# Cross-attention and routed feed-forward attention: first-layer banks, the order at the start of the last stage, tables by kind, and seven batches of k gathered early

## The chip, the cores and the metric

One core of one Trainium2 chip runs the whole kernel in one launch. The metric is device time in microseconds of one execution, as the median of several. The engines are TensorE (PE, with its weight loads as PEld), VectorE (DVE), ScalarE (ACT), GpSimd (POOL) and SyncE (SP, which here only issues DMAs).

## What is computed

x and ctx are 16 batches of 256 tokens of 256 numbers, float32.

```python
x = x + xattn(layernorm(x), ctx, ctx, w_q, w_k, w_v, w_o)       # 16 heads, causal
xn = layernorm(x)
q, k, v = (fff(xn, *tree) for tree in ("q", "k", "v"))          # three trees
attn = softmax(q @ k.T / sqrt(256))
out = x + attn @ v
def fff(x, node_w, node_b, w1, b1, w2, b2):                     # each token goes to one of 16 leaves
    leaf = ...                                                  # 4 decisions, score >= 0
    return relu(x @ w1[leaf] + b1[leaf]) @ w2[leaf] + b2[leaf]  # 256 -> 64 -> 256
```

## The kernel before, in words

The kernel has four stages. Each engine has its own hand-written order; semaphores tie them together.

The attention stage (0 to about 400 us) goes batch by batch: cross-attention, layer norm, the routing decisions of the three trees, and an allocation that gives each token a row in xs_dram, sorted by leaf into pages of 128 rows. POOL scatters the normalised tokens there (indirect DMAs, 128 rows of 1 KB each). SP also loads the leaf tables: for tree 0 in `first_weights`, one of eight parts a batch, and for trees 1 and 2 in `load_table`, four parts each; two parts of tree 2 come during the feed-forward loop (after the stores of quads 3 and 7). A leaf's table row holds W2 = 128 numbers of the first layer and 257 of the second with a bias, side by side (WROW = 385); a part goes with one DMA for the first layer and two for the second.

The feed-forward loop handles 36 quads, 12 per tree, of four pages each. SP loads a quad's rows (`load_quad`, 512 KB) and stores its outputs (`store_quad`, 512 KB). PE's part per quad is `block_T` (transposes of xb, L816), `block_h` (first layer, L827) and `block_out` (second layer, L842 and L846). ACT copies the transposes (`copy_xT`, L1036), applies `relu` (L1043) and copies the outputs (`copy_y`, L1050). VectorE copies each page's leaf weights out of the tables (`take_weights`, L1401 and L1402). Quads go in pairs on PE: T, T of the next pair, out, out of this one, h, h of the next; ACT goes likewise with copy_xT, copy_xT, copy_y, copy_y, relu, relu. In the text a pass is one such turn of six blocks.

PSUM has eight banks, four pairs. Quads' transposes alternate between `pairs[0]` and `pairs[1]` (banks 0 to 3), outputs between `pairs[2]` and `pairs[3]` (banks 4 to 7), and the first layers use banks 4 and 5, the pair of the even quads' outputs. Hence block_h waits for the copy of the even quad's output (y_sb), and block_out for both quads' relus (h_sb).

POOL gathers the loop's outputs from ys_dram back into token order (indirect DMAs, one for 128 rows, L1606): all 32 of q, and then k for the first KB = 9 batches, 18 gathers. They start at quad 14; `after_sixth` ties each to an event of PE so that they are spread over the loop. k's first KFIRST = 5 batches count on one semaphore (k_in), later ones by pairs of batches (k_late).

The last stage is softmax attention over 16 batches, four buffers deep for v and x1 (U = 4): `transposes` of q and k (L877), `scores` (L888), `probs_T` (L898), `values` (L909) on PE; `copy_qT` (L1072) and `exps` (L1080) on ACT; `copy_kT` (L1419), `maxima` (L1424, L1428), `copy_pT` (L1434) and `finish` (L1445) on VectorE. PE starts it only when all outputs are copied (y_sb = 36), because these banks are the same eight. In `finals`, the step of batch b issues transposes of b + 2, probs_T of b, scores of b + 1, values of b - 1. POOL gathers the remaining rows of k (`late_row`, L1606) and all of v (`v_row`, L1638) beside it: first two late rows, the second after the first scores, then v's rows of batch 0, then in each step one late row and two rows of v. SP loads x1 (L503) after v's first rows have landed.

## Time and profile before

| | us |
|---|---|
| median of 3 runs (lowest, highest) | 662.35 (658.48, 664.43) |
| the profiled execution | 668.17 |
| its span | 666.2 |
| PE busy | 589.8 (89%) |
| DVE busy | 441.0 (66%) |
| ACT busy | 295.5 (44%) |
| POOL busy | 236.9 (36%) |
| DMA moved, mean rate | 169.58 MB, 255 GB/s |

Busy times overlap, so they don't add up; PE's is the sum over its instructions with modelled ends. The span is from the first to the last record of the profile, and the execution's time has about 2 us around it. "Releaser" or "<-" behind a row names what ended the engine's idle time before it; "remote" is an event whose sender the profile could not name. The granted clock is the share of 2.4 GHz that TensorE got: 1.00 is its upper level, 0.50 its lower one.

### The profile page before, as it was taken

Reading aid. Unit: us, or ns where it says so; the run is one execution under the profiler, and the core shown is the slowest. Engines: PE = TensorE matmul, PEld = TensorE weight load, DVE = VectorE, ACT = ScalarE, POOL = GpSimd, SP = SyncE. Lnnn points to the kernel's source line nnn. Section 1 sums busy time; section 2 is a strip of 40 time slices with the busy share of each in tenths; the row PEclk is TensorE's granted clock in tenths of the full one; section 3 lists DMA queues with packets and bytes.
Section 4 is the critical chain, followed back from the end, with each engine's and each line's share of the span. In section 5 each row is a group of like instructions: output and inputs, shape, how many; then the busy total and the mean of one; then the engine's idle time right before and its main releaser. Section 6 shows DMA issues by size and latency. Waiting matters only on the chain.

```text
span 666.2 us, 14743 instructions
## 1 busy us (share of the span) xinstructions
PE 589.8 (89%) x5131; PEld 505.4 (76%) x5131; DVE 441.0 (66%) x1511; ACT 295.5 (44%) x482; POOL 236.9 (36%) x298
## 2 busy tenths in 40 slices
PE   7578998998999999999899967759998888689996
PEld 6467787887888887878777856648887777579895
DVE  2765687887889888988788865564554544056664
ACT  3105454443445444545344532017886667333231
POOL 5700011223323432433233144540006556466642
PEclk8869999998999999999799988679999999799999
DMA  6798887889789988988867488758999998656663
GB/s 188 230 301 246 257 265 213 252 261 292 226 272 298 268 270 266 305 245 273 262 204 221 159 260 253 192 189 303 340 376 374 373 373 308 205 172 183 191 189 126
DMA packets 99639, 169.58 MB, mean 255 GB/s; under 512 B 12848, under 2 KB 67824, under 8 KB 99568
## 3 DMA queue, kind: packets, MB, share of 16 engines
q1 hardware_dynamic: 87712, 141.83, 67.7%
q0 software_dynamic: 9216, 25.18, 12.4%
q10 hardware_dynamic: 2640, 1.65, 0.9%
q8 instruction: 41, 0.67, 0.4%
q14 instruction: 30, 0.25, 0.1%
HBM read 92.59 MB, written 75.50 MB: 252 GB/s over the span
## 4 chain that ended last, share of the span: by engine, by line
PE 45%; SPq 16%; DMA 16%; issue 10%; DVE 6%; ACT 3%; another core or an unknown queue 2%; POOL 1%; ACTq 1%; DVEq 0%; POOLq 0%
DMA parts_dram<-k_lo 6%; SPq L334 6%; PE banks L827 5%; PE banks L816 4%; PE banks L888 4%; PE banks L842 4%; DMA parts_dram<-q_lo 3%; PE banks L547 3%; PE banks L909 3%; DMA k<-parts_dram 3%; PE banks L559 3%; PE banks L532 3%; DVE mneg L1184 2%; PE banks L682 2%; PE banks L877 2%
## 5 line engine op out<-in xcount | busy, mean ns | idle before, releaser
L1547 POOL DMA_INDIRECT xs_dram<-xn2s,place x96 | 95.3, 993 | 177.4 <-ACT pt L942 144.9
L942 ACT ACTIVATE pt<-banks 128x768 f32<-128x768 f32 x128 | 103.6, 811 | 108.8 <-PE banks L560 84.3
L1184 DVE TENSOR_REDUCE mneg<-banks 128x2 f32<-128x512 f32 x240 | 122.0, 550 | 37.3 <-PE banks L548 31.7
L547 PE MATMUL banks<-k,q 107*128 107x256 f32 x240 | 76.7, 371 | 18.9 <-DVE mneg L1184 9.0
L559 PE MATMUL banks<-q,k 109*128 109x256 f32 x256 | 75.3, 346 | 1.9 <-DMA q<-m_lo 0.2
L547 PEld LDWEIGHTS banks<-k,q 107*128 107x128 f32 x240 | 46.7, 195 | 30.3 <-DMA k<-parts_dram 11.1
L575 PE MATMUL banks<-pt,vp 128*32 128x256 f32 (+1 forms) x1024 | 54.9, 332 | 4.7 <-ACT pt L942 3.0
L560 PE MATMUL banks<-q,k 109*128 109x128 f32 x256 | 57.8, 226 | 0.0
L1606 POOL DMA_INDIRECT q_all<-ys_dram,place x32 | 31.3, 978 | 71.4 <-PE banks L816 52.6
L559 PEld LDWEIGHTS banks<-q,k 109*128 109x128 f32 x256 | 49.6, 194 | 6.7 <-ACT pt L942 5.9
L548 PE MATMUL banks<-k,q 107*128 107x128 f32 x240 | 54.4, 227 | 0.0
L560 PEld LDWEIGHTS banks<-q,k 109*128 109x128 f32 x256 | 50.4, 197 | 0.1
L1534 POOL TENSOR_SCALAR ve<-mv 128x2 f32<-128x2 f32 x32 | 7.4, 230 | 118.6 <-DVE mv L1110 79.5
L1036 ACT COPY xbT<-banks 128x1024 f32<-128x1024 f32 x36 | 34.9, 1018 | 30.8 <-PE banks L816 30.3
L1401 DVE COPY wb<-tables 128x128 f32 x96 | 21.0, 219 | 41.4 <-PE banks L846 33.3
L548 PEld LDWEIGHTS banks<-k,q 107*128 107x128 f32 x240 | 47.5, 198 | 0.5
L842 PE MATMUL banks<-wb,hT 64*128 64x256 f32 x288 | 42.4, 389 | 5.8 <-ACT hT L1043 3.3
L575 PEld LDWEIGHTS banks<-pt,vp 128*32 128x32 f32 x1024 | 26.8, 109 | 24.0 <-issue 6.0
L1050 ACT COPY yb<-banks 128x1024 f32<-128x1024 f32 x36 | 36.4, 1015 | 18.2 <-remote 11.3
L816 PE MATMUL banks<-ident,xb 128*128 128x128 f32 x288 | 37.5, 285 | 6.9 <-DMA xb<-xs_dram 6.9
L827 PE MATMUL banks<-xbT,wb 128*64 128x128 f32 x576 | 37.3, 282 | 5.1 <-issue 2.3
L827 PEld LDWEIGHTS banks<-xbT,wb 128*64 128x64 f32 x576 | 33.2, 142 | 10.2 <-issue 10.1
(177 smaller groups left out, 1310.5 us busy)
## 6 DMA issues: line engine op xcount, KB each, us to landing
ys_dram<-yb SPq DMA_DIRECT2D x36, 512.0 KB
xb<-xs_dram SPq DMA_DIRECT2D x35, 512.0 KB
k<-parts_dram SPq DMA_DIRECT2D x128, 128.0 KB, 4.3
q<-parts_dram SPq DMA_DIRECT2D x64, 256.0 KB, 4.2
xs_dram<-zero SPq DMA_DIRECT2D x45, 256.0 KB
xs_dram<-zero SPq DMA_DIRECT2D x18, 384.0 KB, 4.4
tables<-leafw SPq DMA_DIRECT2D x16, 257.0 KB
xt<-x SPq DMA_DIRECT2D x16, 256.0 KB
```

Source lines behind the costliest of these rows:

```text
L334: sp.dma_start(full[s][2 * DK * x:2 * DK * (x + 1), hs, :].bitcast(FP).rearrange("p h k -> p (h k)"), src).then_inc(stacked[r][s], 16)
L547: mm(ps[:, 0:S], q[0:KN, t, P:S], k[0:KN, t, :], start=True, stop=True)
L548: last = mm(ps[:, S:S + P], q[0:KN, t, 0:P], k[0:KN, t, 0:P], start=True, stop=True)
L559: mm(ps[:, 0:S], k[0:KM, t, 0:P], q[0:KM, t, :], start=True, stop=True)
L560: last = mm(ps[:, S:S + P], k[0:KM, t, P:S], q[0:KM, t, P:S], start=True, stop=True)
L575: last = mm(W_BANKS[par][32 * g:32 * g + 32, c * S + kt * P:c * S + S], vp[u][:, kt, t, :], pt[:, t, 0:S] if kt == 0 else pt[:, t, S:S + P ...
L816: last = nc.tensor.transpose(pairs[w % 2][:, c, m * P:m * P + P], xb[w][:, m, c * P:c * P + P], ident[:])
L827: last = mm(banks[4 + q % 2][e * HID:(e + 1) * HID, r * P:r * P + P], wb1[(2 * q + r) % UP][:, e, c * HID:c * HID + HID], xbT[q % 2][:, c, ...
L842: mm(pairs[2 + q % 2][:, e, r * D:r * D + D], hT[q % 2][half, r, :], wb2[(2 * q + r) % UP][half, 0:D], start=True, stop=False)
L942: nc.scalar.activation(pt[:, 2 * p:2 * p + 2, :], st_banks(b, p)[:, :, 0:S + P], ACT.Exp, scale=SC).then_inc(exp_sb, 1)
L1184: last = nc.vector.tensor_reduce(mneg[1 - u][:, t, 2 * j:2 * j + 2], S_BANKS[:, :, cols], axis=AX.X, op=ALU.max, negate=True)
L1547: gp.indirect_dma_start(xs_dram[tree], bass.IndirectOffsetOnAxis(ap=place[:, k:k + 1], axis=0), xn2s[m % RING][:, t, :], None).then_inc(sc ...
```

## The change

1. The first layers go to banks 2 and 3, the pair of the odd quads' transposes. block_h waits for both quads' xbT copies and no longer for yb. block_out waits for its own quad's relu. block_T of an odd quad waits for the relus of the pair before.
2. PE's and ACT's order at the start of the last stage: batch 0's transposes go ahead of the last two second layers, its scores right behind them, batch 1's transposes and scores follow, and the waits for yb come one by one before the first two probs_T. VectorE copies kT of batches 0 and 1 first and then takes the maxima.
3. Each table is two runs: all leaves' first layers, then all leaves' second layers.
4. KB = 7 and KFIRST = 3: 14 gathers of k in the loop. The 18 late rows come one and two by turns in the steps of the last stage, none ahead of v's first rows.

```diff
-KB = 9
-KFIRST = 5
+KB = 7
+KFIRST = 3
...
+        whole = [wl0[:]] + [tables[:, t * LEAVES * WROW:(t + 1) * LEAVES * WROW] for t in range(2)]
+        w1s = [w[:, 0:LEAVES * W2].rearrange("p (l n) -> p l n", l=LEAVES) for w in whole]
+        w2s = [w[:, LEAVES * W2:LEAVES * WROW].rearrange("p (l n) -> p l n", l=LEAVES) for w in whole]
...
-                sp.dma_start(wl[t][:, ls, 0:W2], leafw1[t, :, ls, :]).then_inc(wt_late[t], 16)
+                sp.dma_start(w1s[t][:, ls, :], leafw1[t, :, ls, :]).then_inc(wt_late[t], 16)
...
                 ge(pe, xbT_sb, q - 1)
+                if q % 2 == 1:
+                    ge(pe, h_sb, 2 * (q - 1))
...
-                ge(pe, y_sb, 2 * (q // 2) - 1)
+                ge(pe, xbT_sb, 2 * (q // 2 + 1))
...
-                            last = mm(banks[4 + q % 2][e * HID:(e + 1) * HID, r * P:r * P + P],
+                            last = mm(banks[2 + q % 2][e * HID:(e + 1) * HID, r * P:r * P + P],
...
-                pe.wait_ge(h_sb, 4 * (q // 2 + 1))
+                pe.wait_ge(h_sb, 2 * (q + 1))
...
-            pe.wait_ge(y_sb, Q)
...
+                    if i * U + u < 2:
+                        pe.wait_ge(y_sb, Q - 1 + i * U + u)
                     probs_T(i, u)
-                    if u + 1 < U or more:
+                    if (u + 1 < U or more) and i * U + u > 0:
                         scores(i + (u + 1) // U, (u + 1) % U)
...
                 if q + 2 < Q:
                     block_T(q + 2)
                     block_T(q + 3)
+                else:
+                    transposes(0, 0)
                 block_out(q)
                 block_out(q + 1)
...
             scores(0, 0)
             transposes(0, 1)
+            scores(0, 1)
...
                 if q + 2 < Q:
                     copy_xT(q + 2)
                     copy_xT(q + 3)
+                else:
+                    copy_qT(0, 0)
                 copy_y(q)
                 copy_y(q + 1)
...
-            copy_qT(0, 0)
+            copy_qT(0, 1)
             exps(0, 0)
-            copy_qT(0, 1)
...
+                    if i * U + u == 0:
+                        maxima(0, 1)
                     copy_pT(i, u)
-                    if u + 1 < U or more:
+                    if (u + 1 < U or more) and i * U + u > 0:
                         maxima(i + (u + 1) // U, (u + 1) % U)
...
             copy_kT(0, 0)
+            copy_kT(0, 1)
             maxima(0, 0)
-            copy_kT(0, 1)
...
-            gp.wait_ge(tq_ps, 1)
-            late_row(0)
-            gp.wait_ge(s2_ps, 1)
-            late_row(1)
...
+            late = 0
             for b in range(NB - 1):
-                if b + 2 < (NB - KB) * T:
-                    gp.wait_ge(tq_ps, min(b + 3, NB))
-                    late_row(b + 2)
+                for _ in range(1 + b % 2):
+                    if late < (NB - KB) * T:
+                        gp.wait_ge(tq_ps, min(b + 3, NB))
+                        late_row(late)
+                        late += 1
```

## Rows read from the trace of the kernel before

**Rows 1.** Stages: length; PE, PEld, DVE, ACT, POOL busy; clock; DMA share; GB/s
```profile
480.00:500.00 20.00, 19.71 (x232) 17.39 (x228) 10.22 (x48) 16.30 (x26) 1.14 (x2) 1.00 1.05 376
520.00:540.00 20.00, 17.90 (x210) 15.73 (x210) 10.29 (x48) 14.04 (x22) 12.12 (x14) 1.00 1.00 361
...
600.00:620.00 20.00, 20.00 (x121) 18.01 (x120) 12.59 (x30) 7.38 (x25) 11.59 (x13) 1.00 0.65 186
...
575.00:580.00 5.00, 3.05 (x11) 2.50 (x12) 0.69 (x1) 1.60 (x2) 2.84 (x3) 0.50 0.79 228
...
590.00:592.00 2.00, 1.38 (x9) 1.28 (x10) 0.00 (x0) 1.15 (x5) 1.09 (x2) 1.00 1.03 360
```
**Rows 2.** The chain that ended last, by engine
```profile
PE 45%; SPq 16%; DMA 16%; issue 10%; DVE 6%; ACT 3%; another core or an unknown queue 2%; POOL 1%; ACTq 1%; DVEq 0%; POOLq 0%
```
**Rows 3.** PE's timeline, one pass at full pace: start us, length us, engine, line, operation
```profile
469.30 1.97 PE L827 MATMUL banks<-xbT,wb 128*64 128x128 f32 x32
471.20 1.97 PE L816 MATMUL banks<-ident,xb 128*128 128x128 f32 x16
473.09 0.70 PE L842 MATMUL banks<-wb,hT 64*128 64x256 f32 x4
...
474.85 0.60 PE L842 MATMUL banks<-wb,hT 64*128 64x256 f32 x4
...
475.66 0.55 PE L827 MATMUL banks<-xbT,wb 128*64 128x128 f32 x6
```
**Rows 4.** ACT's timeline, the same pass (x2: two instructions merged)
```profile
471.31 0.62 ACT L1043 ACTIVATE hT<-banks,wb 128x128 f32<-128x128 f32 x2 [0.25 <-PE banks L827]
...
474.50 2.11 ACT L1050 COPY yb<-banks 128x1024 f32<-128x1024 f32 x2 [0.25 <-PE banks L846]
```
**Rows 5.** PE's timeline with gathers beside it: first, second and last pass
```profile
501.10 2.18 PE L827 MATMUL banks<-xbT,wb 128*64 128x128 f32 x32
...
508.23 1.97 PE L827 MATMUL banks<-xbT,wb 128*64 128x128 f32 x32 [0.43 <-ACT yb L1050]
...
513.29 0.70 PE L842 MATMUL banks<-wb,hT 64*128 64x256 f32 x4 [1.20 <-issue]
...
567.32 1.97 PE L827 MATMUL banks<-xbT,wb 128*64 128x128 f32 x32 [0.38 <-issue]
```
**Rows 6.** ACT's and POOL's timelines in the pass at 508.23
```profile
509.41 1.01 ACT L1050 COPY yb<-banks 128x1024 f32<-128x1024 f32 x1 [1.32 <-remote]
...
512.62 0.63 ACT L1043 ACTIVATE hT<-banks,wb 128x128 f32<-128x128 f32 x2 [1.67 <-remote]
...
512.85 0.94 POOL L1606 DMA_INDIRECT q_all<-ys_dram,place  x1 [1.01 <-remote]
```
**Rows 7.** PE's timeline at the turn into the last stage
```profile
576.07 1.12 PE L877 MATMUL banks<-ident,q_all 128*128 128x128 f32 x4 [3.40 <-ACT yb L1050]
...
578.92 3.75 PE L888 MATMUL banks<-tables 128*128 128x256 f32 x8 [0.88 <-DVE tables L1419]
...
596.25 0.66 PE L898 MATMUL banks<-ident,tables 128*128 128x128 f32 x4 [0.64 <-ACT tables L1080]
```
**Rows 8.** ACT's, POOL's and DVE's timelines at the turn
```profile
575.01 1.01 ACT L1050 COPY yb<-banks 128x1024 f32<-128x1024 f32 x1 [2.38 <-remote]
...
584.19 0.95 POOL L1638 DMA_INDIRECT tables<-ys_dram,place  x1 [0.30 <-issue]
...
592.98 0.69 DVE L1419 COPY tables<-banks 128x512 f32<-128x512 f32 x1 [3.48 <-remote]
```
**Rows 9.** ACT's and PE's timelines in two steps of the last stage
```profile
604.88 0.47 ACT L1080 ACTIVATE tables<-banks,tables 128x256 f32<-128x256 f32 x1
...
605.88 0.60 PE L898 MATMUL banks<-ident,tables 128*128 128x128 f32 x4
...
610.65 0.60 PE L898 MATMUL banks<-ident,tables 128*128 128x128 f32 x4
```
**Rows 10.** One line: its issues, ns least/median/most, first and last start
```profile
L355 SPq DMA_DIRECT2D tables<-leafw x16: 602/638/1049, 384.4 to 478.2; - x16
```

More of the change, by code:

```diff
@@ L848, in block_out @@
                 last.then_inc(y_ps, 1)
-            block_T(0)
-            block_T(1)
-            block_h(0)
-            block_h(1)
-            for q in range(0, Q, 2):
-                if q + 2 < Q:
-                    block_T(q + 2)
-                    block_T(q + 3)
-                block_out(q)
-                block_out(q + 1)
-                if q + 2 < Q:
-                    block_h(q + 2)
-                    block_h(q + 3)
-            pe.wait_ge(y_sb, Q)
             def transposes(i, u):
@@ L922, in finals @@
                         values((i * U + u - 1) // U, (u - 1) % U)
-            transposes(0, 0)
+            block_T(0)
+            block_T(1)
+            block_h(0)
+            block_h(1)
+            for q in range(0, Q, 2):
+                if q + 2 < Q:
+                    block_T(q + 2)
+                    block_T(q + 3)
+                else:
+                    transposes(0, 0)
+                block_out(q)
+                block_out(q + 1)
+                if q + 2 < Q:
+                    block_h(q + 2)
+                    block_h(q + 3)
             scores(0, 0)
             transposes(0, 1)
+            scores(0, 1)
             finals(0, True)
@@ L1052, in _, with copy_qT @@
             Q = TREES * QUADB
+            def copy_qT(i, u):
+                b = i * U + u
+                act.wait_ge(tq_ps, b + 1)
+                ge(act, s2_ps, b - 1)
+                nc.scalar.copy(qT[u % 2][:], banks[0][:]).then_inc(qT_sb, 1)
             copy_xT(0)
@@ L1065, in _ @@
                     relu(q + 3)
-            def copy_qT(i, u):
-                b = i * U + u
-                act.wait_ge(tq_ps, b + 1)
-                ge(act, s2_ps, b - 1)
-                nc.scalar.copy(qT[u % 2][:], banks[0][:]).then_inc(qT_sb, 1)
             def exps(i, u):
@@ L1399, in take_weights @@
                     leaf = v.snap(leaf_of[page], min_val=0, max_val=LEAVES - 1)
-                    here = wl[tree][:, bass.ds(leaf, 1), :].rearrange("p o n -> p (o n)")
-                    nc.vector.tensor_copy(wb1[u % UP][:, e, :], here[:, 0:W2]).then_inc(w_cp, 1)
-                    nc.vector.tensor_copy(wb2[u % UP][half, :], here[half, W2:WROW]).then_inc(w_cp, 1)
+                    first = w1s[tree][:, bass.ds(leaf, 1), :].rearrange("p o n -> p (o n)")
+                    second = w2s[tree][half, bass.ds(leaf, 1), :].rearrange("p o n -> p (o n)")
+                    nc.vector.tensor_copy(wb1[u % UP][:, e, :], first).then_inc(w_cp, 1)
+                    nc.vector.tensor_copy(wb2[u % UP][half, :], second).then_inc(w_cp, 1)
             leaf_of = [v.alloc_register(f"leaf_of{n}") for n in range(2 * XB)]
```

12 lines of the change are left out of this document (5 added, 7 removed).

## Prediction

> **What bounds the kernel now.** The stage table comes first [rows 1], then the shares of the chain that ended last [rows 2], then the timelines of single engines where the diff works. TensorE (PE) is the largest holder of the chain. The change touches three stretches: the feed-forward loop (about 448 to 573 us, 18 passes of two quads, L859 to L871), the turn into the last stage (573 to 596) and the last stage itself.
>
> At full pace a pass takes 475.66 - 469.30 = 6.36 us [rows 3]: first layers 1.90, transposes 1.89, second layers 0.66 + 3 x 0.55 = 2.31 (473.09 to 475.40), and 0.26 in which PE stands. ACT's timeline says why: the first of the two yb copies runs from 474.50 to 475.51 [rows 4], and block_h waits for it (y_sb), since its banks are those of the even quad's output.
>
> From 501.10 on, while GpSimd gathers, the passes take (567.32 - 501.10) / 9 = 7.36 us [rows 5], so 9 us are lost over nine passes. PE doesn't wait for loads of xb there. It stands before the second layers (1.20 us at 513.29), for the relu at 512.62, and that relu starts 2.5 us after the modelled end of its matmuls (508.23 + 1.90 = 510.13); POOL, gated on the same event, starts 0.23 us behind it [rows 5, 6]. So PE's events are seen late. That isn't so at full pace, where a relu starts at 471.31 for matmuls that end at 471.20 [rows 3, 4]. DMA is full in both stretches (376 and 361 GB/s) [rows 1]; only the gathers are new.
>
> At the turn, the last yb copy starts at 575.01 [rows 8], the first transposes at 576.07 after 3.40 us of idle, and the granted clock is 0.50 from 575 to 580, its lower level: scores take 3.75 us instead of 1.89 [rows 1, 7]. The rows of v are first gathered at 584.19, behind a late row of k that waited for the first scores [rows 8]. The regular pace begins with the transposes of batch 2's probabilities at 596.25 [rows 7]. From there a batch takes 610.65 - 605.88 = 4.77 us [rows 9] and PE is busy without a break [rows 1].
>
> **First layers in banks 2 and 3.** (a) Removed: block_h's wait for yb, and block_out's wait for the other quad's relu. At full pace this gives back 0.26 us in the 8 passes before 501.10 that carry no gathers: -2.1. The work next in line doesn't take it: with the first layers 0.26 earlier ACT ends the yb copies at 476.6 and the relus by 477.97, and PE needs the second at 478.25. (b) Added: the odd quad's transposes now wait for both relus (h_sb), and behind them in PE's order stand both second layers. At full pace the second relu ends 471.31 + 0.62 = 471.93 and the odd transposes start at 471.20 + 0.95 = 472.15 [rows 3, 4], a margin of 0.2 us: no cost. In the gathering stretch that margin is gone: the relu ends at 513.25, so the 0.95 us of odd transposes would follow it instead of lying before it, and the second layers start at 514.25 instead of 513.29. Against this +0.95 stands the freed wait (0.43 before the pass at 508.23 [rows 5]): net +0.5 to +0.7 a pass, +4.5 to +6 over nine. That is one end. The other: in this stretch DMA is full, a pass moves 4 x 0.524 MB and about 4.5 gathers of 0.131 MB, 2.69 MB, which at some 370 GB/s is 7.3 us, all that was measured. If the late events come from gathers upon full queues, a slower pass relieves them, and what remains is the traffic: 46 gathers instead of 50 before the end, 4 x 0.131 MB / 0.37 = -1.4. No row tells which; I take the middle, +1.8, and keep -1.4 to +6.
>
> **Tables by kind.** The same bytes are moved in the same number of DMAs, in longer runs (one per partition instead of one per leaf). An issue for a second-layer piece takes 0.64 us [rows 10]; each still is one instruction on the SP queue, so I count no gain there. VectorE's two copies per leaf keep their sizes. Cost 0; bounds -2 (a tenth of the 0.64 us off each of the 32 second-layer issues, all of it on SP's share of the chain [rows 2]) and +0.5. By the Trainium skill ("DMA: Bandwidth & Descriptors", section "Why small descriptors are slow (HBM only)") a packet carries a fixed overhead of about 3 cycles: by that a first-layer piece of 512-byte runs would be some 12% quicker, an estimate of 0.1 us each. The trace shows no landing time for these pieces; the sum would not change.
>
> **The turn.** I lay out the new order with the old durations, from the end of the last first layers at 569.2.
> - PE: transposes of batch 0 to 570.2, in the stall that was before the second layers. They need q and six gathers of k; the sixth is gated on quad 33's first layers (562.6) and so lands some 3 us ahead. Second layers to 572.75, scores of batch 0 (warm, 1.75) to 574.5, transposes of batch 1 to 575.4.
> - ACT: qT of batch 0 behind the relus (570.75), the two yb copies, the second still at 575.01, qT of batch 1 to 576.6. PE: scores of batch 1 576.65 to 578.4, transposes of batch 2 to 579.3, probabilities of batch 0 to 579.75, transposes of batch 3 to 580.5. VectorE: kT of batch 2, maxima of batch 1 to 580.9; ACT: exps to 581.9. PE: probabilities of batch 1 to 582.3, scores of batch 2 to 584.05.
> - POOL: the last store of ys is issued at 576.4 and lands by 580; v's rows go then, no longer behind a late k row, and land at about 584.6. Values of batch 0 end at 586.3, transposes of batch 4 at 587.2, and batch 2's probabilities follow.
>
> Against 596.25 that is 9.0 us earlier. I take off 1.5: when the x1 loads land beside gathers, DMA is full (1.03 at 590 to 592) and an event of PE (kT of batch 3, transposed by 589.3) was seen only at 592.98 [rows 1, 8]. In the new order this falls on 586 to 590, where VectorE also may wait for x1 in finish before it copies kT of batch 4. So -7.5, between -4 and -10.
>
> Here the clock matters. In the trace a stand of 3.4 us came with the lower level [rows 1, 7], and stands of 1.2 us in the loop did not [rows 5]. The new order's longest stands are 1.25 and 1.4 us, so I count on the upper level. The Trainium skill ("TensorE: Matmul & The Clock Gate", section "What's actually happening") says that the throttled state is the default and activity releases it. By that, short gaps in a row could still lose it; 8.9 us of PE's work between 576.65 and 587 would then take up to twice as long, and the gain would fall to some 3 us.
>
> **Late rows of k.** 18 instead of 14 of them fall in the last stage, one and two by turns, so POOL issues 3.5 gathers a batch at 0.95 + 0.30 us: 4.4 of the 4.77 available. A batch with four takes 5.0 and the next makes up for it; k rows come two batches ahead of their use, v rows one. +0.5. Unknown: whether bursts of four make PE's events late here too. The slack is small: exps end at 604.88 + 0.47 = 605.35, and the probabilities' transposes start at 605.88 [rows 9], so 0.5 us. DMA is at 0.65 of full here, with 3 gathers a batch, and no event is late [rows 1]. So I keep 0 to +13.
>
> **Sum.** -2.1 + 1.8 - 7.5 + 0.5 = -7.3 us. On the profiled execution (668.17, span 666.2) that is 660.9. The median of the runs is 5.8 us lower, with the same work; I take the difference from it: 662.35 - 7.3 = 655.0.
>
> **Rivals.**
> 1. The loop loses the whole wait. For: PE stood at the second layers in five of the nine passes. Against: full DMA explains the pace as well. Loop -2.1 + 6 = +3.9, turn -7.5, rest +0.5: 659.2.
> 2. The turn's gain is mostly lost: the clock falls at the short stands, or k's rows land late. Loop -0.3, turn -3, rest +0.5: 659.5.
> 3. Everything hidden stays hidden: loop -2.1 - 1.4, turn -9.5: 649.3.
> 4. Slower: in the last stage the events of scores are late whenever gathers run in bursts. Place: VectorE's maxima, exps, then PE's probs_T, in the 12 batches that carry late rows. Price: lateness less 0.5 of slack; with 1.8 us, 12 x 1.3 = +15.6, so 655.0 + 15.6 = 670.6. It decides from 1.1 us of lateness (12 x 0.6 eats 7.3). For: 1.3 to 3.8 us were seen in the loop and at 592.98. Against: none with three gathers at 0.65 of DMA.
>
> **Chances.** Forecast 0.46 (its own range 651 to 659), rival 1 0.24, rival 2 0.08, rival 3 0.11, rival 4 0.11. The range 649 to 664 leaves out rival 4 and half of rival 3. A measurement can tell about 1% (6.6 us, so 655.7 and 669) from no change. Forecast, two thirds below that bound, and rival 3 give faster 0.42; rival 4 gives slower 0.11 (its nearer cases included); 0.47 within.
>
> **What would show it.** Passes at full pace of 6.1 us, with no idle before L827; passes in the gathering stretch of 7.0 to 7.7, with the idle now before the odd transposes (L816) for relu; first scores ahead of the last yb copy's end and at 1.9 us; v's first row near 580; the regular pace 7 to 9 us earlier; 4.77 us a batch held. Wrong: passes of 8 us or more; clock 0.50 after 575; idle before probs_T in the last stage.

## The result, and the profile after

The changed kernel takes 667.18 us in the median of 16 runs (661.83 to 670.63), the kernel before 663.5 in 16 runs (658.48 to 675.53) on the same chip. The ratio is 1.0061, with a 95% interval of 1.0033 to 1.0089. Forecast were 655.0 us and a range of 649 to 664: the time lies outside it, on the slow side. Ratios and intervals, here and below, leave out executions more than 1.5% above the fastest of the same kernel; where that changes a reading, the median of all is given beside it.

The profiled execution of after took 665.63 us, its span is 663.7; that of before 668.17 and 666.2. So the two profiles stand the other way round than the medians, by 2.5 us against 3.7. Single executions lie up to 12 us from the median (675.53), the profiled one of before 4.7 above it and that of after 1.6 below, and I therefore read the profiles by stage. h(0) and h(34) are the first "first layers" of the first and of the last pass of the loop; the turn ends where batch 2's probabilities are transposed.

| us | before | after |
|---|---|---|
| loop, h(0) to h(34) | 448.71 to 567.32: 118.6 | 448.68 to 563.63: 114.95 |
| turn | to 596.25: 28.9 | to 584.65: 21.0 |
| last stage, to the span's end | 69.95 | 79.05 |

The stages of after, by the view of windows (length; PE, PEld, DVE, ACT, POOL busy; clock; DMA share; GB/s), to be laid beside [rows 1]:

```profile
480.00:500.00 20.00, 20.00 (x234) 17.75 (x234) 10.61 (x51) 16.79 (x26) 1.59 (x2) 1.00 1.03 383
520.00:540.00 20.00, 17.43 (x204) 14.92 (x201) 10.65 (x48) 13.59 (x23) 10.90 (x12) 1.00 1.02 393
575.00:580.00 5.00, 3.67 (x28) 3.12 (x27) 2.71 (x6) 2.85 (x10) 2.84 (x3) 1.00 0.26 73
590.00:592.00 2.00, 1.06 (x8) 0.85 (x8) 1.97 (x7) 0.24 (x1) 1.42 (x2) 1.00 0.61 187
600.00:620.00 20.00, 18.70 (x107) 16.38 (x106) 11.46 (x26) 5.64 (x20) 12.52 (x14) 1.00 0.67 191
```

Two things changed sides. At 575 to 580 the granted clock is 1.00, where it was 0.50. And in 600 to 620, where PE was busy for all 20.00 us, it now stands for 1.3. The DMA share there is nearly the same, 0.67 for 0.65.

PE's timeline of one pass at full pace, for [rows 3]:

```profile
469.53 1.97 PE L830 MATMUL banks<-xbT,wb 128*64 128x128 f32 x32
471.43 1.97 PE L819 MATMUL banks<-ident,xb 128*128 128x128 f32 x16
473.32 0.70 PE L845 MATMUL banks<-wb,hT 64*128 64x256 f32 x4
...
475.71 1.53 PE L830 MATMUL banks<-xbT,wb 128*64 128x128 f32 x24
```

The pass takes 6.18 us and nothing waits. With gathers beside it (for [rows 5]), the nine passes from 500.48 to 563.63 take 7.02 us each, and PE now stands in the middle of the transposes, for the relu, at the place where the new wait is:

```profile
500.48 1.97 PE L830 MATMUL banks<-xbT,wb 128*64 128x128 f32 x32
...
510.93 1.06 PE L819 MATMUL banks<-ident,xb 128*128 128x128 f32 x8 [0.72 <-ACT hT L1047]
...
514.32 1.97 PE L830 MATMUL banks<-xbT,wb 128*64 128x128 f32 x32
...
563.63 1.97 PE L830 MATMUL banks<-xbT,wb 128*64 128x128 f32 x32
```

PE's waits, in sum (total us, times, longest):

```profile
PE banks L885 <- ACT tables L1086: 7.9, 7, 1.7
...
PE banks L819 <- ACT hT L1047: 5.3, 6, 2.1
...
PE banks L830 <- ACT xbT L1040: 1.2, 1, 1.2
```

The last is the loop's first pass: block_h now waits for both xbT copies, and there is no work yet to cover that. It comes before h(0), so the loop's length in the table doesn't hold it. The first is the one that matters: the probabilities' transposes wait for exps, seven times. Four of these stands are new and lie in the last stage (1.74, 1.54, 0.95 and 1.72 us); one of 1.33 belongs to the turn, and two of 0.31 at the very end are in the kernel before too. PE's timeline shows where (the counterpart of [rows 7] and [rows 9]):

```profile
570.53 1.97 PE L875 MATMUL banks<-tables 128*128 128x256 f32 x8 [0.26 <-DVE tables L1425]
...
579.86 0.63 PE L885 MATMUL banks<-ident,tables 128*128 128x128 f32 x4 [1.33 <-ACT tables L1086]
...
584.65 0.60 PE L885 MATMUL banks<-ident,tables 128*128 128x128 f32 x4
...
590.02 0.63 PE L864 MATMUL banks<-ident,q_all 128*128 128x128 f32 x4 [1.32 <-issue]
...
592.83 0.66 PE L885 MATMUL banks<-ident,tables 128*128 128x128 f32 x4 [1.74 <-ACT tables L1086]
...
599.36 0.66 PE L885 MATMUL banks<-ident,tables 128*128 128x128 f32 x4 [1.54 <-ACT tables L1086]
```

Scores start at 570.53 at full clock, and batch 2's probabilities at 584.65, 11.6 us ahead of 596.25. Then the steps, from one batch's probabilities to the next, take 8.18, 6.53, 5.33, 5.94, 4.82, 4.77, 4.96 and 6.70 us to 631.88. Eight steps at 4.77 would be 38.2; they are 47.2. That is all of the 9.1 us by which the last stage grew: 5.2 of it in the two steps right behind the turn, 3.9 in the six after them.

ACT's, VectorE's and POOL's timelines say what held the first of these (the number in brackets is the idle time before the row and its releaser; "remote" names no sender):

```profile
589.29 0.59 ACT L1061 COPY tables<-banks 128x512 f32<-128x512 f32 x1 [5.09 <-remote]
```
```profile
589.35 0.69 DVE L1425 COPY tables<-banks 128x512 f32<-128x512 f32 x1 [1.96 <-remote]
```
```profile
576.46 0.94 POOL L1646 DMA_INDIRECT tables<-ys_dram,place  x1 [3.72 <-DMA ys_dram<-yb]
...
586.47 0.95 POOL L1646 DMA_INDIRECT tables<-ys_dram,place  x1 [0.30 <-issue]
589.53 0.94 POOL L1614 DMA_INDIRECT k_all<-ys_dram,place  x1 [2.11 <-remote]
```

Three engines wait for one thing, the transposes of batch 4, which PE had run by 584.21 + 0.60 = 584.8. All three go on between 589.29 and 589.53, 4.5 us later. POOL had issued nine gathers back to back from 576.46 to 587.42. With qT and kT late, the scores of that batch, its exps and its probabilities are late in turn.

### The profile page after: what moved, and what is told of

Same layout as the page of the kernel before. It is cut to its first block, busy times and chain, and to the rows that moved or that the text cites. A ratio compares the mean times of both kernels' runs of the same rounds, so it can differ in the third digit from the quotient of the medians.

```text
span 663.7 us, 14747 instructions
## 1 busy us (share of the span) xinstructions
PE 589.4 (89%) x5131; PEld 501.1 (76%) x5131; DVE 441.3 (66%) x1511; ACT 295.2 (44%) x482; POOL 236.2 (36%) x298
## 2 busy tenths in 40 slices
DMA packets 91448, 169.58 MB, mean 256 GB/s; under 512 B 12849, under 2 KB 56561, under 8 KB 91377
## 4 chain that ended last, share of the span: by engine, by line
PE 44%; DMA 15%; SPq 12%; DVE 10%; issue 8%; another core or an unknown queue 6%; ACT 3%; POOL 1%; DVEq 0%; ACTq 0%; POOLq 0%
DMA parts_dram<-k_lo 6%; PE banks L830 5%; PE banks L819 5%; PE banks L845 5%; SPq L335 4%; DMA k<-parts_dram 4%; PE banks L533 4%; PE banks L548 3%; PE banks L560 3%; PE banks L875 3%; DMA parts_dram<-q_lo 3%; DVE mneg L1189 2%; PE banks L683 2%; PE banks L576 2%
## 5 line engine op out<-in xcount | busy, mean ns | idle before, releaser
L576 PE MATMUL banks<-pt,vp 128*32 128x256 f32 (+1 forms) x1024 | 57.0, 341 | 4.0 <-ACT pt L946 4.0
L819 PE MATMUL banks<-ident,xb 128*128 128x128 f32 x288 | 39.6, 288 | 12.4 <-DMA xb<-xs_dram 6.7
L819 PEld LDWEIGHTS banks<-ident,xb 128*128 128x128 f32 x288 | 32.8, 147 | 18.1 <-issue 10.6
L1646 POOL DMA_INDIRECT tables<-ys_dram,place x32 | 30.3, 946 | 25.0 <-issue 6.9
```

The source lines that it names most:

```text
L576: last = mm(W_BANKS[par][32 * g:32 * g + 32, c * S + kt * P:c * S + S], vp[u][:, kt, t, :], pt[:, t, 0:S] if kt == 0 else pt[:, t, S:S + P ...
L819: last = nc.tensor.transpose(pairs[w % 2][:, c, m * P:m * P + P], xb[w][:, m, c * P:c * P + P], ident[:])
```

## The experiments

There are eighteen runs, on five chips. These are of two kinds, and every reading below needs that: on three of them (chips 11, 12 and 2) the kernel before takes 634 to 637 us, on two (13 and 5) 663 to 666, and the chip of the first comparison is of the second kind with its 663.5. I call them the quick and the slow kind. The stages of the profiles:

| kernel (chip) | ratio to before, same chip | loop | turn | last stage |
|---|---|---|---|---|
| before_again (13) | 1 (one run) | 117.8 | 28.2 | 70.0 |
| after_third (13) | 1.0116 (1.0066 to 1.0165) | 117.2 | 21.1 | 81.5 |
| paced_again (13) | 1.0016 (0.9963 to 1.0070) | 117.1 | 21.1 | 81.4 |
| u_late_third (13) | 1.0008 (0.9966 to 1.0051) | 119.2 | 25.0 | 72.9 |
| no_late (5) | 0.9885 (0.9839 to 0.9931) | 118.1 | 22.1 | 69.0 |
| b_late (5) | 1.0044 (1.0009 to 1.0078) | 115.2 | 26.1 | 76.3 |
| v_first (5) | 1.0005 (0.9968 to 1.0042) | 120.4 | 19.9 | 78.5 |
| vx_spread_again (5) | 0.9975 (0.9939 to 1.0011) | 116.9 | 19.7 | 76.0 |
| after_again (11) | 0.9976 (0.9946 to 1.0007) | 107.0 | 19.4 | 70.3 |
| u_tables (11) | 0.9968 (0.9932 to 1.0003) | 106.8 | 20.1 | 70.6 |
| u_late_again (11) | 0.9934 (0.9896 to 0.9973) | 108.6 | 20.5 | 69.9 |
| o_banks (12) | 1.0014 (0.9983 to 1.0046) | 107.7 | 24.0 | 69.8 |
| u_banks (12) | 0.9909 (0.9876 to 0.9942) | 109.3 | 19.5 | 70.3 |
| u_late (12) | 0.9905 (0.9874 to 0.9937) | 107.0 | 20.7 | 70.3 |
| paced (12) | 0.9882 (0.9838 to 0.9926) | 108.5 | 19.6 | 74.1 |
| x_spread (2) | 0.9909 (0.9878 to 0.9939) | 106.8 | 19.8 | 70.3 |
| vx_spread (2) | 0.9897 (0.9854 to 0.9940) | 107.2 | 19.4 | 69.8 |
| ux_spread (2) | 0.9928 (0.9895 to 0.9961) | 108.3 | 19.7 | 69.8 |

The ratios are of many runs, the stages of one execution each. The profiled executions of paced and u_late_third lie 6 and 8 us above the median of all their kernel's, those of after_third and b_late 6 below; so single stages are compared, not their sums.

### The banks, in and out (o_banks, u_banks)

o_banks is the kernel before with the change's first part alone; u_banks is after with that part undone:

```diff
-                if q % 2 == 1:
-                    ge(pe, h_sb, 2 * (q - 1))
...
-                ge(pe, xbT_sb, 2 * (q // 2 + 1))
+                ge(pe, y_sb, 2 * (q // 2) - 1)
...
-                            last = mm(banks[2 + q % 2][e * HID:(e + 1) * HID, r * P:r * P + P],
+                            last = mm(banks[4 + q % 2][e * HID:(e + 1) * HID, r * P:r * P + P],
...
-                pe.wait_ge(h_sb, 2 * (q + 1))
+                pe.wait_ge(h_sb, 4 * (q // 2 + 1))
...
```

> The kernel before with the bank change alone. Theory 1: passes of 6.2 and 7.0 us, the turn and the last stage as before: 660 us, 3 to 4 us under the kernel before. Rival A: 3 us or more above it. My own first forecast of this part was about even (from -3.5 to +4).

> The changed kernel with the first layers back in banks 4 and 5 with their old waits, all else kept. Theory 1, with the bank change as a gain: a pass at full pace 6.36 us instead of 6.19, passes beside gathers about 7.3 instead of 7.0, so 3 to 4 us slower than the changed kernel: 670 to 671 us. Rival A: faster than the changed kernel, 663 us or less.

The banks alone give 1.0014, so nothing that the interval can tell. All of after but the banks gives 0.9909 on a quick chip, within the intervals of u_late and paced on the same chip, which have them; after itself was not run there. A pass is 6.18 instead of 6.36 us, eighteen times 0.17 would be 3 us, and the loop of u_banks is 2.4 us longer than after_again's (109.3 and 107.0). Of that the wait of 1.2 us ahead of h(0) gives back half, and what is left is too little to be seen in 635 us. These runs speak for the quick kind only.

### The late rows as before (u_late, u_late_again, u_late_third)

```diff
-KB = 7
-KFIRST = 3
+KB = 9
+KFIRST = 5
...
+            gp.wait_ge(tq_ps, 1)
+            late_row(0)
+            gp.wait_ge(s2_ps, 1)
+            late_row(1)
...
-                for _ in range(1 + b % 2):
-                    if late < (NB - KB) * T:
-                        gp.wait_ge(tq_ps, min(b + 3, NB))
-                        late_row(late)
-                        late += 1
+                if b + 2 < (NB - KB) * T:
+                    gp.wait_ge(tq_ps, min(b + 3, NB))
+                    late_row(b + 2)
```

> The changed kernel with its fourth part undone: nine batches of k gathered in the loop, five on the first semaphore, and POOL's last-stage order as before (one late row a step, two ahead of v). Theory 1 (runs of gathers without a wait between them make PE's events late in the last stage): the stands before probs_T, some 9 us in the profile of the changed kernel, shrink to under 2 us, while the turn loses some 4 us since v's rows wait again behind the second late row; 659 to 663 us, below the changed kernel's 667. Rival A (the bank change costs the time, in the loop): 667 as the changed kernel, stands in the last stage or not. Rival B (tables by kind cost it, ahead of the loop): 667 too.

> The changed kernel with nine batches of k gathered in the loop and POOL's order as before, once more. Theory 2: on a chip with about 637 for the kernel before, equal to the changed kernel within 2 us; on one with about 663, 3 to 7 us faster than the changed kernel. Rival B: equal on both.

> The changed kernel with nine batches of k gathered in the loop and POOL's order as before. Where the kernel before takes about 663: 3 to 7 us faster than the changed kernel, its stands before probs_T under 2 us. Where it takes about 635: equal or up to 3 us faster (it was 0.9905 and 0.9934 of the kernel before in the first two calls, the changed kernel 0.9976 in the second).

On the slow chip the time falls from 1.0116 to 1.0008, about 7 us (by the medians of all executions 5.1, from 671.69 to 666.58); in its profile the last stage is 72.9 instead of 81.5, and the turn 25.0 instead of 21.1. The two large steps of the turn's end are still there, 9.86 and 7.81 us where after_third has 9.17 and 7.55; the first of them now lies ahead of batch 2's probabilities and is booked to the turn. What is gone are the later ones: every step behind them takes 4.77 us or less. On quick chips the ratio is 0.9905 (chip 12) and 0.9934, beside 0.9976 for after itself on the second one's chip. So GpSimd's part of the change costs some 1% on the slow kind; on chip 11 the difference of 0.4% lies within the intervals.

### The changed kernel again (after_again, after_third, before_again)

> The changed kernel once more, on the chip of this call. The four kernels before ran on another chip than the blind comparison: there the kernel before took 637 us instead of 663, DMA reached 415 GB/s beside the gathers instead of 373, and no event of PE came late. Theory 2 (the sign hangs on the chip: where DMA reaches over 400 GB/s the change gains, where it stops near 380 its denser gathers make events late): if the kernel before takes about 637 here, the changed one takes 629 to 632 with no stand before probs_T over 0.5 us once the last stage is in its pace; if it takes about 663, the changed one takes 666 to 669 with stands of 5 us or more in total. Rival C (the stands come from POOL's order alone): stands on either chip.

> The changed kernel, third chip or a chip seen before. Theory 2: 0.990 to 0.998 of the kernel before where that takes about 635, 1.003 to 1.009 where it takes about 663, then with stands before probs_T of 5 us or more. Rival C: stands on any chip.

The same kernel is 0.9976 on chip 11 and 1.0116 on chip 13. What differs is seen in after_again's windows (one beside the loop's gathers, one of the last stage) and in PE's passes:

```profile
500.00:520.00 20.00, 20.00 (x236) 17.59 (x234) 12.33 (x55) 16.98 (x26) 13.35 (x14) 1.00 1.03 414
...
590.00:610.00 20.00, 19.79 (x118) 17.56 (x117) 12.66 (x29) 6.93 (x24) 12.73 (x14) 1.00 0.67 207
```
```profile
507.14 1.97 PE L830 MATMUL banks<-xbT,wb 128*64 128x128 f32 x32
...
513.34 1.97 PE L830 MATMUL banks<-xbT,wb 128*64 128x128 f32 x32
```

DMA moves 414 GB/s at the same full share, where the slow kind's profiles have 360 to 394 in the same 20 us; the passes take 6.20 us with 14 gathers in 20 us beside them; in the whole trace no wait is put down to "remote". The turn has the same clash, 335 GB/s at a share of 1.00 from 557 to 559 with gathers back to back, and no event is late. POOL even issues 33 gathers without a break there, from 549.4 to 591.0. So a run of gathers alone doesn't make events late; it takes the slow kind too.

In after_third the clock falls as well. PE stands 1.69 us before 588.23 and 1.75 us before 591.04, with batch 5's transposes between; then its scores take 3.62 us instead of 1.89. The two steps from 581.87 take 9.17 and 7.55 us. Its windows in the first stand and at the fall:

```profile
586.00:588.00 2.00, 0.55 (x3) 0.14 (x1) 0.43 (x1) 0.49 (x1) 0.26 (x1) 1.00 0.76 230
...
590.00:592.00 2.00, 0.95 (x5) 0.96 (x6) 0.53 (x2) 1.47 (x5) 1.45 (x2) 0.50 0.49 149
```

The same loss is in the loop, at the place of the change's new wait. In after_third PE stands 2.25 us before the odd quad's transposes, for a relu that ACT started after 1.66 us of "remote"; then the granted clock is 0.50 from 529.5 to 531.7, second layers that take 0.60 us take 1.06, and the pass takes 10.24 us. PE's timeline and the window:

```profile
527.95 1.56 PE L819 MATMUL banks<-ident,xb 128*128 128x128 f32 x8 [2.25 <-ACT hT L1047]
...
530.67 1.06 PE L845 MATMUL banks<-wb,hT 64*128 64x256 f32 x4
```
```profile
529.50:531.70 2.20, 2.20 (x13) 1.86 (x14) 0.00 (x0) 1.01 (x1) 0.94 (x1) 0.50 1.03 354
```

no_late, paced_again and v_first have it in the same pass (10.30, 10.27 and 9.93 us). The kernel before, before_again and b_late, with the old banks, never fall below 1.00 in those passes; nor does after, which stands 2.10 us there and takes 8.47 us for the pass.

before_again is the base of the table's rows of chip 13:

> The kernel before, unchanged, for a profile on the chip of this call. Theory 2: on a chip where it takes about 635 no event of PE is late (no idle time whose releaser has no name), the passes of the loop are 6.36 us with gathers too, and from the last first layers to batch 2's probabilities it takes some 24 us, against 19.4 in the changed kernel. On a chip where it takes about 663: passes of 7.4 us and nameless waits of some 55 us over the engines, as in the profile shown.

### The tables (u_tables)

```diff
...
-        w1s = [w[:, 0:LEAVES * W2].rearrange("p (l n) -> p l n", l=LEAVES) for w in whole]
-        w2s = [w[:, LEAVES * W2:LEAVES * WROW].rearrange("p (l n) -> p l n", l=LEAVES) for w in whole]
+        w1s = [w[:, :, 0:W2] for w in wl]
+        w2s = [w[:, :, W2:WROW] for w in wl]
```

> The changed kernel with the tables interleaved again, leaf by leaf. Forecast of the prediction: same time as the changed kernel within 2 us (cost 0, bounds -2 and +0.5). Rival B: 3 us or more faster than the changed kernel. A rival the other way: slower by 1 to 3 us, if the longer runs ease the queues in the first passes of the loop, where two parts of the third table still come in.

0.9968 beside 0.9976: no difference. The profiles count 99,640 packets with the tables interleaved and 91,448 by kind, so 8% fewer packets brought nothing that the intervals can tell. This is the quick kind only.

### Every second late row moved behind v's rows (paced, paced_again)

```diff
-                for _ in range(1 + b % 2):
-                    if late < (NB - KB) * T:
-                        gp.wait_ge(tq_ps, min(b + 3, NB))
-                        late_row(late)
-                        late += 1
+                if late < (NB - KB) * T:
+                    gp.wait_ge(tq_ps, min(b + 3, NB))
+                    late_row(late)
+                    late += 1
...
+                if b % 2 == 1 and late < (NB - KB) * T:
+                    gp.wait_ge(o_ps, b)
+                    late_row(late)
+                    late += 1
```

(the second block stands behind the step's last row of v.)

> The changed kernel with the second late row of every other step moved behind v's second row and gated on an output of values, so that POOL stands between it and the others. Theory 1: the stands before probs_T go down from 9 us to some 2 to 4 us (the backlog at the turn stays a run of gathers), 660 to 664 us. Rivals A and B: 667 us, nothing changes.

> The changed kernel with every second late row kept apart by a wait for values. Theory 1 (runs of gathers delay PE's events) holds only where events are late at all: about 663 for the kernel before, then 3 to 6 us faster than the changed kernel. Elsewhere equal to it within 2 us; one profile showed a stand of 2.4 us for k's rows, so it could also be 1 to 2 us slower.

The edit was meant to part the run of four, and it doesn't: the moved row's gate is open when POOL comes to it, and the next step's row follows at once. In paced_again POOL issues five gathers without a break and then waits for a late event (POOL's timeline):

```profile
609.96 0.94 POOL L1614 DMA_INDIRECT k_all<-ys_dram,place  x1 [1.36 <-PE banks L864]
...
614.96 0.95 POOL L1614 DMA_INDIRECT k_all<-ys_dram,place  x1 [0.30 <-issue]
617.46 0.94 POOL L1646 DMA_INDIRECT tables<-ys_dram,place  x1 [1.55 <-remote]
```

The steps are as long as in after_third (9.86 and 7.29 us behind the turn, later ones up to 6.80), and so is the last stage, 81.4. The ratio is 1.0016 beside after's 1.0116 on that chip, but the medians of all executions are 670.44 and 671.69 us, 1.2 us apart. So these runs don't test shorter runs of gathers, and no gain from the edit is shown on the slow chip. On the quick chip it is 0.9882. There the profile shows another cost of late rows: PE stands 2.36 us for a row of k that hasn't landed, in a step of 7.91 us. after_third and paced_again have such a stand too, 1.78 and 1.76 us.

### The late rows left out (no_late)

The transposes of batch b read the k of batch b mod 7, so the kernel leaves out nine batches of k:

```diff
...
-                                                       src[:, b, t * D + c * P:t * D + c * P + P], ident[:])
+                                                       src[:, b if src is q_all else b % KB, t * D + c * P:t * D + c * P + P], ident[:])
...
-                for _ in range(1 + b % 2):
-                    if late < (NB - KB) * T:
-                        gp.wait_ge(tq_ps, min(b + 3, NB))
-                        late_row(late)
-                        late += 1
```

> The changed kernel without the 18 late rows of k: transposes of batch b read the k of batch b mod 7, so the k of nine batches is left out and POOL has two gathers a step. Theory 1': on a slow chip the last stage falls to 70 to 71 us and the turn stays at 21, 655 to 658 us. Rival D: one or two stands of 3 us and more stay right behind the turn, last stage 74 us or more. On a fast chip: the changed kernel's time within 1 us.

0.9885 on a slow chip (660.01 us in the median of all, 5.5 under before); 18 gathers' traffic is gone too, so it bounds the cost rather than prices it. POOL's longest run is five gathers, at the turn, and the step there takes 5.78 us. From 593.72 on each step takes 4.77 us (PE's timeline):

```profile
588.90 0.66 PE L885 MATMUL banks<-ident,tables 128*128 128x128 f32 x4 [0.83 <-ACT tables L1086]
593.72 0.60 PE L885 MATMUL banks<-ident,tables 128*128 128x128 f32 x4
598.49 0.60 PE L885 MATMUL banks<-ident,tables 128*128 128x128 f32 x4
```

The x1 loads are still there, and still meet v's rows.

### Only the denser rows (b_late)

The kernel before, with its order at the turn, and:

```diff
-KB = 9
-KFIRST = 5
+KB = 7
+KFIRST = 3
...
+            late = 2
...
-                if b + 2 < (NB - KB) * T:
-                    gp.wait_ge(tq_ps, min(b + 3, NB))
-                    late_row(b + 2)
+                for _ in range(1 + b % 2):
+                    if late < (NB - KB) * T:
+                        gp.wait_ge(tq_ps, min(b + 3, NB))
+                        late_row(late)
+                        late += 1
```

> The kernel before with seven batches of k gathered in the loop and one or two late rows a step; order of the turn, banks and tables as before. Theory 1': on a slow chip the turn stays at 28 us and the last stage grows by 4 us or more, 665 to 670 us (1.00 to 1.01). Rival D: the last stage stays within 2 us of 70, 661 to 664. On a fast chip: as the kernel before within 1 us.

1.0044, and the last stage 76.3 instead of 70. So the denser rows cost 6 us of that stage, with the order at the turn, the banks and the tables as they were. The loop and the turn are 2 to 3 us shorter each, with four gathers fewer in the loop, and the time is only 2 to 3 us longer. One step of it in the whole timeline (PEld left out by the dots):

```profile
600.04 0.66 PE L898 MATMUL banks<-ident,tables 128*128 128x128 f32 x4
...
603.52 0.69 DVE L1434 COPY tables<-banks 128x512 f32<-128x512 f32 x1 [2.81 <-remote]
603.75 0.95 POOL L1638 DMA_INDIRECT tables<-ys_dram,place  x1 [1.57 <-remote]
...
606.18 0.66 PE L898 MATMUL banks<-ident,tables 128*128 128x128 f32 x4 [1.15 <-ACT tables L1080]
```

PE transposed the probabilities by 600.70. VectorE, which had stood for 2.81 us, and POOL, which waits for the same event before a row of v, both saw it at 603.5 to 603.8. VectorE's copy is 2.8 us late, its maxima after it too, and PE stands at the next probabilities.

### The old number of rows, the new turn (v_first)

```diff
-KB = 7
+KB = 9
...
-                for _ in range(1 + b % 2):
+                for _ in range(2 if b in (3, 6) else 1):
```

> The changed kernel with nine batches of k in the loop (14 late rows, two in two of the steps and one in the others), v's first rows still ahead of all late rows. Theory 1' (where the chip makes PE's events late at all, the cost grows with POOL's gathers per batch in the last stage): where the kernel before takes about 663, turn 21 us as in the changed kernel, last stage 71 to 74 us instead of 79 to 81, so 657 to 661 us, below both kernels. Rival D (the cost is a clash at the turn, which comes with the earlier start whatever the density): last stage stays near 78 and the time near 667. Where the kernel before takes about 635: 0.990 to 0.996, like the changed kernel or 2 us better.

```profile
588.05 0.60 PE L885 MATMUL banks<-ident,tables 128*128 128x128 f32 x4
597.41 1.11 PE L885 MATMUL banks<-ident,tables 128*128 128x128 f32 x4 [1.86 <-ACT tables L1086]
605.07 0.60 PE L885 MATMUL banks<-ident,tables 128*128 128x128 f32 x4
609.84 0.60 PE L885 MATMUL banks<-ident,tables 128*128 128x128 f32 x4
```

Two large steps, 9.36 and 7.66 us, right behind the turn, with the clock lost in between (1.11 us for a row of 0.60), then 4.77. So there are two costs: the clash at the turn comes with the new order even at the old number of rows, and the density costs further on. The time is that of before, 1.0005: the turn's gain is given back.

v_first also holds the nearest thing to a test of the run's length. Behind the two large steps POOL issues three gathers a batch and the steps take 4.77 us. One time it issues five in a row (614.60 to 620.56); then it waits 1.54 us for "remote", and the step from 619.37 takes 5.70.

### The loads of x1 spread out (x_spread, vx_spread, ux_spread, vx_spread_again)

```diff
             for u in range(U):
+                if u > 0:
+                    sp.wait_ge(pT_ps, u + 1)
                 load_x1r(0, u)
```

in after, in v_first and in u_late.

> The changed kernel, but the x1 loads of batches 1, 2 and 3 (0.26 MB each) no longer go out in one burst with batch 0's: each waits for the probabilities of batch 1, 2 and 3 to be transposed. In the profile of after, DMA was full from 582 to 586 (four x1 loads beside four gathers), and three engines saw an event of PE 4 to 5 us late, together, at 589.3 to 589.5; the two steps behind it took 8.18 and 6.53 us instead of 4.77. Theory A (the lateness at the turn comes of the burst of x1 loads upon the gathers): on a chip where the kernel before takes some 665 us these two steps fall to 5.5 us or less, the last stage from 79 to 75, the time is 3 to 5 us under the changed kernel's, so 0.999 to 1.003 of before. Rival B (any five or more gathers in a row make the events late, whatever else is loaded): the stands stay, 1.006 to 1.012. On a chip where before takes some 635 us both expect what after gave there, 0.995 to 1.000.

> v_first (the new order at the turn, k of nine batches gathered in the loop, one late row a step and two in two of them) with the same spread x1 loads. v_first had two stands right behind the turn (steps of 9.36 and 7.66 us, the clock at 0.50 between them) and none later. Theory A: these go, the last stage falls from 78.5 to 71 or 72, and the whole is 0.988 to 0.994 of before: it would beat both kernels on either kind of chip. Rival B: 1.000 as v_first. If only the clock is saved: 0.995 to 0.997.

> u_late (the new order at the turn, GpSimd's order of before: two late rows ahead of v's first rows) with the spread x1 loads. u_late gave 1.0008 where before takes some 665 us, its turn 25.0 and its last stage 72.9. Theory A: the last stage falls to 70.5 to 71.5 and the turn stays, 0.995 to 0.999. Rival B: nothing changes, 1.000.

> vx_spread once more, for a chip on which the kernel before takes some 665 us (the first one took 636 there, and nothing was to be told apart). There, theory A (burst of x1 loads upon gathers): steps behind the turn of 5.5 us or less, last stage 71 to 72, 0.988 to 0.994 of before. Rival B (run of gathers alone): two stands as in v_first, last stage 77 to 79, 1.000. If only the clock is saved: 0.995 to 0.997. On a chip of the other kind: 0.990 again.

The first three fell on a quick chip, where nothing was to be told apart. The last fell on chip 5, v_first's: 0.9975, where v_first had 1.0005. PE's steps from 583.12 on are 8.55 and 6.51 us, then 4.77:

```profile
583.12 0.60 PE L887 MATMUL banks<-ident,tables 128*128 128x128 f32 x4
591.67 0.66 PE L887 MATMUL banks<-ident,tables 128*128 128x128 f32 x4 [1.98 <-ACT tables L1088]
598.18 0.60 PE L887 MATMUL banks<-ident,tables 128*128 128x128 f32 x4
602.95 0.60 PE L887 MATMUL banks<-ident,tables 128*128 128x128 f32 x4
```

and its windows show DMA at a fraction of full while VectorE waited for the copy of kT that it began at 588.29 after 4.04 us of "remote":

```profile
586.00:590.00 4.00, 2.31 (x14) 1.65 (x12) 1.68 (x4) 0.03 (x1) 1.70 (x2) 1.00 0.23 68
590.00:594.00 4.00, 2.33 (x10) 1.99 (x11) 2.70 (x7) 1.50 (x5) 3.03 (x4) 0.82 0.66 150
```

The stands are 2 us shorter in sum and remain, and the clock is still lost (0.50 from 594 to 596). PE had transposed k of batch 4 by 583.3, so VectorE saw it 5.0 us late. The DMA share was 0.93 in 582 to 584, when the event was due, and 0.47 and then 0.23 while it was awaited. The edit parts the burst only in half: SP issues two of the four loads together at 580.28 and the third at 589.00. So a burst of four isn't needed for the stands, but two x1 loads beside the run of gathers remain. Against them speaks no_late, which has all four in a burst and gathers in a row only up to five, and loses 1.0 us there (a step of 5.78 us). Theory A's forecast of steps of 5.5 us or less fails. The rival had the stands right; its last stage of 77 to 79 and its 1.000 are missed a little, with 76.0 and 0.9975.

vx_spread is also the best on both kinds together: 0.9897 on a quick chip, and 0.9975 on a slow one, where the interval (0.9939 to 1.0011) doesn't rule out no gain.

## Why the prediction was wrong

**The step that failed is "Late rows of k: +0.5", and with it "I take off 1.5" at the turn.** Both are terms of the sum, and both failed by one mechanism: on this kind of chip, events of PE are seen late once gathers stand in a row.

The first term let the gathers cost POOL's time alone and rested the rest on "no event is late" at three gathers a batch and 0.65 of the DMA share. Behind the turn's two steps it measured 3.9 us in after and 4.4 in after_third, 6.3 in b_late, where the denser rows stand alone, and not +0.5. (Of the 4.4, 2.0 fall in the step in which PE stood for a row of k that hadn't landed; that wait the term had at nothing too.) The mechanism is that of rival 4, given a chance of 0.11: place (maxima, exps, probs_T) and cause (runs of gathers) are as written there. The lateness is larger than its 1.8 us (4.5 behind the turn, 2.8 in b_late), but fewer batches are hit: six steps of after are more than 0.1 us over 4.77, not twelve. The argument against rival 4 was the DMA share, and that was no measure of it: the share hardly rose (0.67) and the steps grew. What changed with the edit was the number of gathers a batch, three to 3.5, and how many stand in a row, up to five and at the turn nine. Which of the two counts isn't shown, but for the one step of v_first.

The second term is the larger miss. I laid out POOL's start at the turn but not its backlog: v's rows, the late rows whose gates had already opened, v's next rows, 9 x 1.25 us without a break. The late event that I moved to 586 to 590 did come there, and cost 3.4 us in its step and 1.8 in the next (4.4 and 2.8 in after_third) instead of 1.5. It falls behind probs_T(2), so that the stage table books it to the last stage. Together the terms are the 9.1 us by which that stage grew, 11.6 on chip 13. v_first and vx_spread_again keep the second with the old number of rows. On slow chips the lost clock is part of it: 0.50 behind the stands in after_third, paced_again, u_late_third, v_first and vx_spread_again, but not in after.

**The turn, -7.5: right in the number, in part by luck.** 28.9 to 21.0 in the profiles, 28.2 to 21.1 on chip 13, 24.0 (o_banks, the old order) to 19.5 (u_banks, the new one) on the quick chip. Scores ran ahead of the last yb copy, at the upper level of the clock. But the forecast was -9.0 with 1.5 taken off for the late event, and that event lies outside the stretch that was measured: the stretch itself gave 7.9 and 7.1 and not 9.0, and with the event's 5.2 us taken off 2.7 is left. Rival 2 (the clock falls at the short stands) didn't come in the stretch; the clock fell a step later, in the five profiles named above, behind two stands in a row.

**The loop.** At full pace I had 0.26 us a pass and it is 0.18: the other 0.08 stays between the last second layers and the next first layer (475.71), though nothing waits there any more. Eight passes give -1.4 instead of -2.1, and 1.2 of it is taken back ahead of h(0); that wait for both xbT copies I had not counted. Beside the gathers I foresaw the stand before the odd transposes, and it is there (5.3 us in six). The nine passes are 7.02 us each instead of 7.36, -3.1 in sum and so beyond the good end of my -1.4 to +6; on chip 13 they differ by -0.1, and before and after stand 0.6 us apart over the whole loop. Part of that difference is a cost that I had put at nothing: the stand for relu took the clock in after_third and three more profiles, a pass of about 10 us. Rival 1 didn't come. The two runs that isolate the banks show no gain either, on the quick kind.

**The tables, 0: right.** u_tables says so. The Trainium skill ("DMA: Bandwidth & Descriptors", section "Why small descriptors are slow (HBM only)") would have made the longer runs some 12% quicker, as estimated in the prediction; no run here shows a difference in the time.

**The sum.** By stages, the slow kind gets -2 (loop, mean of two pairs), -7.5 (turn) and +10.3 (last stage), +0.8 us. Measured are +3.7 and, on chip 13, +6.0 by the medians. The rest isn't found in the profiles: h(0) alone moves by 6 us from one to the next, both profiles of after are of executions below their median (by 1.6 and 6.4 us), and that of before is 4.7 above its own. It stays open.

**Open, too:** what makes PE's events late on one kind of chip only. The traces show the lateness and what goes with it (back-to-back gathers, 360 to 394 instead of 412 to 415 GB/s at a full share), not the mechanism. No kernel that parts the runs at the same number of gathers, none without GpSimd's gathers, and none with as many gathers of another size was tried.

## What to carry to other kernels

Before moving gathers onto an engine that "has time", look in the trace for "remote" waits: where events are seen 3 us late beside gathers in one stage, count with the same in the next once gathers stand in a row there, even at 0.67 of the DMA share. When a gate in one stage opens earlier, lay out the whole queue behind it, its backlog too, and ask what each consumer of PE's events has for slack (here 0.5 us). And compare on more than one chip: by the same instructions this change is 0.6% and 1.2% slower on two measurements of the slow kind, and 0.9976 (0.9946 to 1.0007) on a quick chip, where variants of it reach 0.990. Last, read in the trace whether an edit did what it was written for: that of paced_again didn't part the gathers.

## What the runs showed of the hardware that was not expected

- Two kinds of chip: 634 to 637 us and 663 to 666 for the same kernel. At a full DMA share beside the loop's gathers (500 to 520 us) they move 412 to 415 and 360 to 394 GB/s.
- On the slow kind events of PE are seen 2.8 us (b_late), 4.5 (after) and 5.0 (vx_spread_again) late, in after by VectorE, ScalarE and GpSimd within 0.25 us of each other (589.29, 589.35, 589.53), during or right behind back-to-back gathers. On the quick kind no such wait stands in any trace, behind 33 gathers in a row either (after_again).
- The lateness outlasts a full DMA: in vx_spread_again the share was 0.93 in 582 to 584, when the event was due, and 0.23 in 586 to 590, while it was still awaited.
- Two stands of 1.69 and 1.75 us with 1.1 us of transposes between them cost the clock in after_third (0.50 from 590 to 596), while two of 1.32 and 1.74 us in after, before 590.02 and 592.83, didn't. In the loop one stand of 2.25 us took it to 0.50 for 2.2 us (after_third, 529.5 to 531.7), one of 2.10 in after didn't. So the margin is small, and the prediction's row at 3.4 us was no guide to it. The fall fits the Trainium skill ("TensorE: Matmul & The Clock Gate", section "What's actually happening"), by which the lower level is the default and activity releases it.
